# Loads of the output accumulators issued by GpSimd instead of SyncE in a cross-attention and feed-forward kernel

## The reference, cut to what matters

```python
x = x + xattn(layernorm(x), ctx_768, Wq, bq, Wk, bk, Wv, bv, Wo, bo)     # x: 8 x 1024 x 512, 16 heads, 64 keys
hidden = layernorm(x) @ W1 + b1                                          # 512 -> 2048
imag = w_imag * sin(theta + hidden * 0.1)
q = hidden + (cos(theta) * w_real + sin(theta) * w_imag) * imag * 0.1
out = x + relu(q) @ W2 + b2                                              # 2048 -> 512
```

## Time and profile before

| | us |
|---|---|
| median of 3 runs (lowest, highest) | 1956.13 (1955.64, 1956.42) |
| the profiled execution: own time | 1956.12 |
| its span | 1953.9 |
| TensorE busy | 1938.4 |
| VectorE, ScalarE, GpSimd busy | 1486.0, 1263.8, 547.1 |

### The profile page before, as it was taken

The page is one execution under the profiler, slowest core; times in us unless marked ns, Lnnn a source line. Parts: engine busy times, 40 slices in busy tenths (PEclk is TensorE's granted clock), DMA queues, the critical chain, the costliest instruction groups (busy, mean ns, idle before and its releaser), DMA issues.

```text
span 1953.9 us, 27911 instructions
## 1 busy us (share of the span) xinstructions
PE 1938.4 (99%) x9156; PEld 1621.8 (83%) x9156; DVE 1486.0 (76%) x2305; ACT 1263.8 (65%) x2132; POOL 547.1 (28%) x390
## 2 busy tenths in 40 slices
PE   9999999999999999999999999999999999999999
PEld 7788888888888888888888888888888888888887
DVE  8988888888876876887577768758757876875763
ACT  6767767667664877677467557647737755764761
POOL 7877777777774221000000000000000000000000
PEclk9999999999999999999999999999999999999999
DMA  7567687687675999789989898997987988898845
GB/s 239 151 185 185 169 211 182 170 215 193 168 159 156 346 336 324 259 275 285 266 288 280 258 297 250 286 291 235 291 277 262 273 262 279 252 286 244 251 151 194
DMA packets 363362, 472.75 MB, mean 242 GB/s; under 512 B 166096, under 2 KB 201936, under 8 KB 363216
## 3 DMA queue, kind: packets, MB, share of 16 engines
q1 hardware_dynamic: 346512, 439.44, 71.5%
q0 software_dynamic: 15840, 31.46, 9.2%
q10 hardware_dynamic: 864, 0.04, 0.0%
HBM read 347.90 MB, written 108.00 MB: 233 GB/s over the span
## 4 chain that ended last, share of the span: by engine, by line
PE 92%; DMA 3%; DVE 2%; POOL 2%; issue 1%; ACT 0%; SPq 0%; POOLq 0%; DVEq 0%; ACTq 0%
PE psum L2011 30%; PE psum L2013 30%; PE psum L2012 30%; PE psum L2104 2%; DMA w_ring<-w1s 1%; POOL prob L977 0%; PE psum L2053 0%; DMA x_dram<-res 0%; POOL prob L956 0%; DVE prob L1639 0%; DVE top L1648 0%; POOL q_lo L909 0%; DVE xt_lo L1748 0%; SPq L586 0%; DMA v_dram<-v_parts 0%
## 5 line engine op out<-in xcount | busy, mean ns | idle before, releaser
L2011 PE MATMUL psum<-w_ring,act_hi 128*128 128x512 f32 x1024 | 398.4, 389 | 0.0
L2012 PE MATMUL psum<-w_ring,act_hi 128*128 128x512 f32 x1024 | 398.4, 389 | 0.0
L2013 PE MATMUL psum<-w_ring,act_lo 128*128 128x512 f32 x1024 | 398.4, 389 | 0.0
L2011 PE MATMUL psum<-xo,w_ring 128*128 128x512 f32 x784 | 305.2, 389 | 1.8 <-DMA w_ring<-w1s 1.8
L2013 PE MATMUL psum<-xo,w_ring 128*128 128x512 f32 x784 | 305.0, 389 | 0.0
L2012 PE MATMUL psum<-xo,w_ring 128*128 128x512 f32 x784 | 305.0, 389 | 0.0
L1829 DVE SCALAR_TENSOR_TENSOR frac<-frac,turns 128x512 f32<-128x512 f32 x256 | 175.3, 695 | 77.1 <-ACT frac L1361 76.7
L2011 PEld LDWEIGHTS psum<-w_ring,act_hi 128*128 128x128 f32 x1024 | 192.2, 188 | 40.0
L2013 PEld LDWEIGHTS psum<-w_ring,act_lo 128*128 128x128 f32 x1024 | 192.2, 188 | 40.0
L1398 ACT ACTIVATE frac<-frac 128x512 f32<-128x512 f32 x256 | 156.1, 626 | 106.9 <-DVE frac L1829 106.9
L2012 PEld LDWEIGHTS psum<-w_ring,act_hi 128*128 128x128 f32 x1024 | 192.2, 188 | 39.8
(11 more groups left out here) (186 smaller groups left out, 4343.3 us busy)
## 6 DMA issues: line engine op xcount, KB each, us to landing
w_ring<-w2s SPq DMA_DIRECT2D x240, 512.0 KB, 4.3
w_ring<-w1s SPq DMA_DIRECT2D x392, 256.0 KB, 4.7
x_sb<-turn_dram SPq DMA_DIRECT2D x58, 512.0 KB, 6.4
res<-in_x SPq DMA_DIRECT2D x64, 256.0 KB, 3.7
x_dram<-res SPq DMA_DIRECT2D x64, 256.0 KB, 3.1
x_dram<-bo_row POOLq DMA_DIRECT2D x16, 1024.0 KB, 10.7
acc<-x_dram SPq DMA_DIRECT2D x16, 1024.0 KB, 7.3
x_sb<-in_x SPq DMA_DIRECT2D x15, 1024.0 KB, 6.3
```

The lines of the kernel that those rows point to most:

```text
L2011: pe.matmul(o, a_hi, b_hi, start=first, stop=False, skip_group_check=resumed)
L2012: pe.matmul(o, a_hi, b_lo, start=False, stop=False, skip_group_check=resumed)
L2013: return pe.matmul(o, a_lo, b_hi, start=False, stop=last, skip_group_check=resumed)
```

## The change

The 16 loads of accumulators leave SyncE's program and are put into GpSimd's, with the same waits. GpSimd issues the load of tile 0 at its step j = 2 ahead of the first sums, that of tile 1 after its last sums, and each later one right ahead of the bias add of the same tile. So a load now goes out as soon as the store of tile T-2 has landed, and the bias add as soon as the load has. The bias of tiles 14 and 15 (`add_bias_rows`) still follows the bias adds of tiles 4 and 6. One of two `rsqrt` of each pair now stands behind the load and the bias add of the odd tile.

```diff
--- before (SyncE)
-            def load_acc(T):
-                if T >= 2:
-                    sp.wait_ge(out_stored[T % 2], 16 * (T // 2))
-                elif T == 1:
-                    sp.wait_ge(w_lo_done, SPLIT0 + FFN_CHUNKS)
-                sp.wait_ge(x1_biased, 16 * (T + 1))
-                sp.dma_start(acc[:, T % 2], x1_rows[T]).then_inc(acc_in[T % 2], 16)
...
                 if j == 2:
                     sp.dma_start(b2_row[:], b2.partition_broadcast(P)).then_inc(b2_in, 16)
-                    load_acc(0)
...
-                if j == 27:
-                    load_acc(1)
...
-                        if name == "P2" and p == 0 and T == 1:
-                            load_acc(2)
...
-                        if name == "P1" and p == 3:
-                            load_acc(2 * T + 1)
...
-                        if more and at == second_half(T, 7):
-                            load_acc(2 * T + 2)
...
+            def load_acc(T):
+                if T >= 2:
+                    pool.wait_ge(out_stored[T % 2], 16 * (T // 2))
+                elif T == 1:
+                    pool.wait_ge(w_lo_done, SPLIT0 + FFN_CHUNKS)
+                pool.wait_ge(x1_biased, 16 * (T + 1))
+                pool.dma_start(acc[:, T % 2], x1_rows[T]).then_inc(acc_in[T % 2], 16)
+
             for j in range(FC + HALF1):
                 pool.wait_ge(turns_done, j + 1)
+                if j == 2:
+                    load_acc(0)
...
+            load_acc(1)
             for T in range(1, FFN_PAIRS):
                 more = T + 1 < FFN_PAIRS
+                load_acc(2 * T)
                 add_last_bias_by_dma(2 * T)
                 if T in (2, 3):
                     add_bias_rows(GUARDED + T - 2)
                 if more:
                     rsqrt(TILES + 2 * T + 2)
+                load_acc(2 * T + 1)
+                add_last_bias_by_dma(2 * T + 1)
+                if more:
                     rsqrt(TILES + 2 * T + 3)
-                add_last_bias_by_dma(2 * T + 1)
```

## The result

| | before | after |
|---|---|---|
| median of 20 runs each (lowest, highest) | 1956.64 (1954.02, 1961.09) | 1960.80 (1957.51, 1966.05) |
| the profiled execution: own time | 1956.12 | 1966.05 |
| its span | 1953.9 | 1963.8 |

The ratio of after to before is 1.0022, with a 95% interval of 1.0016 to 1.0028: the change costs 4.2 us, 3.1 to 5.5. The forecast was +1.9 us; the time lies in its range. The profiled execution of after is 5.2 us above the median of its kernel, so its trace can't be read against the trace of before without saying which part of it belongs to that execution alone.

The account below looks back on a forecast made before the run. TensorE was taken as the bound, waiting only for late weight transfers. Old stalls -1.8, pairs 1 and 2 +1.7 and +1.5, pair 4 +0.5 gave +1.9 us, 1958.0 us, range 1954.0 to 1962.0.

Parts of the forecast that it names:

- What bounds the kernel: TensorE is busy 1938.4 of 1953.9 us, so only weights that arrive after TensorE wants them change the time.
- The limit of 8.0 us: In the second half of a pair, a w2 load must land within 8.0 us of its issue.
- What goes: TensorE's two old waits for w1, near 980 and 1145, vanish: -1.8 us.
- The mechanism and its place: At ends of pairs, earlier bias adds (about 945) delay w2 loads; TensorE waits near 958 to 961 and 1122 to 1125.
- Pairs 1 and 2: w2 loads beside the bias add and the bias of tiles 14 and 15 come late: +1.7 and +1.5 us.
- second rival: Starved queue: w2 loads at pairs 1 and 2 spaced 4.5 us against 2.72 wanted; +5.5, 1961.6 us; chance 0.22.
- Pairs 3, 5 and 6 at nothing: At the ends of these pairs, w2 loads beside a lone bias add are not late: 0 us.
- The first accumulator, the accumulators 1 and 2, the odd ones at 0: Moving these loads to GpSimd, at stage 2's start and in first halves of pairs, costs TensorE 0 us.
- The load on GpSimd's queue at 7.5 us: An even accumulator's plain load takes 7.5 us on GpSimd's queue, so the bias add goes out at about 945.
- no load is late: Rival: w2 loads in second halves stay under 8.0 us and only the old stalls go; 1954.3 us; chance 0.22.
- not early: Rival: GpSimd's load takes 15 us, the bias add starts as late as before, old stalls stay; 1956.1 us; chance 0.06.
- starved queue: Rival: w2 loads behind the first late one at pairs 1 and 2 fall further behind; +5.5, 1961.6 us; chance 0.22.

Follow-up runs that it names:

- e1_bias_late: The changed kernel with GpSimd's bias adds of tiles 4, 6, ... 14 held until sweep 9 of the second half has ended; 1954.18 us, ratio 0.9987 to before.
- e4_rows_late: The kernel before with the bias of tiles 14 and 15 added behind the first `rsqrt` of pairs 2 and 3; 1953.46 us, ratio 0.9984 to before.
- e7_after_rows_late: The changed kernel with only the bias of tiles 14 and 15 moved behind the odd tile's bias add in pairs 2 and 3; 1958.14 us, ratio 1.0010.
- e5_both_late: The changed kernel with bias adds of tiles 4 to 14 held until sweep 9 ends and the bias of tiles 14 and 15 later; 1954.15 us, ratio 0.9990.
- e8_after_again: The changed kernel once more, unaltered, timed against before; 1960.05 us, ratio 1.0019 (1.0009 to 1.0028).

## Why the prediction was right, and where its sum was short

- *What bounds the kernel* held: every gap on TensorE that the change makes or takes away ends with a weight landing.
- *The limit of 8.0 us* held: 7.97 measured.
- *What goes*, -1.8 us for the old stalls: right, they are gone in both traces of after, and of its variants only `e1_bias_late` has 0.3 us of them. The term is nearer -2.3, the mean of three traces. I had put it down to the megabyte of accumulator ahead on SyncE's queue and to the earlier end of GpSimd's two transfers, and each is nearly enough by itself: `e1_bias_late` has only the first and keeps 0.3 us, `e4_rows_late`, which leaves the accumulator where it was, takes one of the two transfers away and keeps nothing.
- *The mechanism and its place*: right. In pair 1 the bias add goes out 13 us behind the store (13.7 forecast), and TensorE waits at 960.35, 963.87, 1128.48 and 1132.91 in the trace of after, near 958 and 1123 in the other.
- *Pairs 1 and 2*, +1.7 and +1.5: 1.8 and 2.7 in one trace, 1.3 and 1.4 in the other. The size was right. The spacing of the second rival was seen once, at pair 2 in the slower trace, where the next load was late again by 1.4 us.
- *Pairs 3, 5 and 6 at nothing*: **this step failed.** "7.8 and 7.9 us at the end of pair 3 ... 7.5 and 7.6 in pair 6. So in pairs 3, 5 and 6 nothing is late". For pair 5 no row was shown. Those w2 loads took 8.95 (pair 3) and 9.16 us (pair 6) in the trace of after, and up to 9.5 us beside a lone bias add in `e7_after_rows_late`. Pair 3 lost 1.0 and 1.1 us, pair 6 1.1 and 0, pair 5 0 and 0.5. I took two or three transfers per pair, all from one execution, for the upper end of what such a load takes, when they stood 0.1 to 0.5 us below the limit; two more executions of the kernel before reach 8.4 us in pair 5 and 8.8 in pair 6. A term that lies so near to its limit has a size other than 0; the runs put it at 0 to 1.1 us for each of three pairs, 1.9 us in total as the mean of the two traces. With the means of the traces in place of the terms, and 0.7 us that the matmuls behind the waits lose, the sum is -2.3 + 3.6 (pairs 1, 2) + 0.3 (pair 4) + 1.9 + 0.7 = +4.2, not +1.9. The time lay in the range because that was wide enough to hold this miss of 2.3 us, not because anything in the sum foresaw it.
- *The first accumulator, the accumulators 1 and 2, the odd ones at 0*: right. GpSimd's issue of a plain load took 0.82 us where I took 1.3; the two `x_sb<-turn_dram` beside these loads and the bias of tile 2 took 12.6 and 10.1 us where I had some 11. The room of 7.7 us was used up: VectorE waited 0.9 us for the second (0.7 in the other trace), TensorE for neither.
- *The load on GpSimd's queue at 7.5 us*: short, with 8.5 us in the middle of 15 loads and 12.2 at most. In pairs 1 to 4 of the trace it took 6.0 to 10.4 us, so the bias add came 1.5 us earlier to 3 us later than forecast, and stayed within the stretch without room.
- The *rivals*: "no load is late" and "not early" are excluded by the traces. The bound of 1970 that goes with the second is wrong by its own terms, -1.8 + 6.8 + 6.8 + 0.5 = +12.3, which is 1968.4; nothing else hangs on it. The "starved queue" had the time (+5.5) nearer than the forecast had, by the wrong way: not more at pairs 1 and 2, but some at each pair.

## What to carry to other kernels

A transfer that nobody waits for still has a time at which it does no harm: before it is moved earlier, look which loads on other queues are then in flight and how much room each has, not only who waits for it. Where loads stand within half a microsecond of their limit in a single trace, don't count them at zero; count the spread of the same transfer over all its places. And a stall in a full stretch goes with any one megabyte that leaves it, so choose the one that can leave without meeting something tighter: `e4_rows_late` gained 3 to 4 us and `e1_bias_late`, the change with its bias add held back, 2.5 to 3, where the change itself drew the bias add along and made new stalls.

## What the runs showed of the hardware that I had not expected

*A plain load slows both queues.* On GpSimd's queue beside w2 the megabyte took 6.0 to 10.9 us, and 12.2 right behind another one (5.9 to 7.9 on SyncE's), and the slowest w2 load beside it 7.9 us (`e1_bias_late`) and 8.1 (`e5_both_late`) in place of 5.7 behind it on one queue (6.8 at most, in `e4_rows_late`).

*The start of stage 2 differs from one execution to the next*, by 1.0 to 6.6 us over the traces, and most of it lies ahead of what the change moves. In the two longest, after and `e1_bias_late`, TensorE's clock falls. Stretches of the trace of after, behind the wait of 2.1 us for `xt_lo` that ends at 631.88, with the granted clock third from the end:

```profile
630.00:632.00 2.00, 0.12 (x1) 0.15 (x2) 1.55 (x3) 0.66 (x2) 0.00 (x0) 0.99 0.71 248
632.00:634.00 2.00, 2.00 (x5) 1.62 (x6) 2.00 (x4) 0.00 (x0) 0.00 (x0) 0.50 0.56 214
...
636.00:637.00 1.00, 1.00 (x6) 0.78 (x6) 0.00 (x0) 0.51 (x1) 0.00 (x0) 1.00 0.78 104
```

At 0.50, which is 1.2 GHz, a matmul starts each 0.43 us and not each 0.23; eight of them cost 1.7 us. The same is in `e1_bias_late` behind 2.7 us without a matmul, and costs 2.9 us there, in a trace that lies 4.3 us above the median of its kernel. The mean granted clock over the whole execution shows just below 1.000 in both (0.999 and 0.998). On the two chips of the experiments that is as frequent in before (11 of 33 executions, 5 of 33) as in its variants (11 of 44, 5 of 42). In the result it is 11 of 20 executions of after, with a median of 1962.71 against 1959.25 of the other nine, and nothing is recorded of before there; so a part of the 4.2 us, under 2, may be chance of this kind. Measured again (`e8_after_again`) the change cost 3.7 us by the ratio, 1.8 to 5.5.

*VectorE beside GpSimd.* In the trace of after one operation of VectorE on two inputs took 2.71 us, where it takes 0.74 or 0.75 in the second trace of after, while GpSimd made its sums:

```profile
645.33 2.71 DVE L1840 SCALAR_TENSOR_TENSOR hid<-frac,gain,hid 128x512 f32<-128x512 f32 x1
...
645.35 1.44 POOL L543 TENSOR_TENSOR sums<-sum_raw 128x256 f32<-128x256 f32 x2
```

The Trainium skill, "GPSIMD Engine Reference", "Specifications", has GpSimd share its way into SBUF with VectorE and names instructions with two SBUF inputs as a case of contention; the trace agrees for this one, but no run separates the two, so it stays an observation.
